# A graph-convolution kernel on one core: the first layer's product with its weights takes float16 halves instead of float32

## The reference, cut to what matters

```python
norm = rsqrt(deg_out[src] * deg_in[dst])
msg = (h[src] @ W1 + h[src] * h[dst] @ W2) * norm[:, None]
out = h @ W1 + segment_sum(msg, dst)
```

## Time and profile before

| | |
|---|---|
| median of 3 runs | 563.75 us (563.54 to 563.83) |
| the profiled execution's own time | 563.75 us |
| its span, first to last instruction | 559.7 us |
| busy: TensorE / VectorE / ScalarE | 493.3 / 423.7 / 247.3 us |
| first layer, first to last L667 | 245.2 to 401.7 us |
| second layer, first to last L673 | 405.5 to 555.6 us |

### The profile page before, as it was taken

One profiled execution on the slowest core, in us unless ns is written; L12 is line 12 of the kernel. 1 busy time (PEld: TensorE's weight loads), 2 busy tenths in 40 slices (PEclk: granted clock), 3 DMA queues, 4 the chain that ended last, 5 costly groups with the idle time before them and its releaser, 6 DMA issues.

```text
span 559.7 us, 19159 instructions
## 1 busy us (share of the span) xinstructions
PE 493.3 (88%) x7774; PEld 457.8 (82%) x7774; DVE 423.7 (76%) x1157; ACT 247.3 (44%) x661; POOL 192.4 (34%) x307
## 2 busy tenths in 40 slices
PE   0294688899797999599999999999999999999995
PEld 0073577687586877499999999999899999999995
DVE  4698469999888798777887787788766666767673
ACT  0285488899796888523223222322211111111111
POOL 3679698879999998400000000000000000000000
PEclk9998699999989799889999999999999999999999
DMA  2166110000000000000000000000000020002011
GB/s 69 52 102 113 53 30 19 7 19 3 19 3 20 2 21 2 1 2 3 3 2 2 4 2 2 2 4 2 3 1 2 4 40 2 3 2 39 3 26 18
DMA packets 19428, 9.87 MB, mean 18 GB/s; under 512 B 16081, under 2 KB 18657, under 8 KB 19342
## 3 DMA queue, kind: packets, MB, share of 16 engines
q1 hardware_dynamic: 18222, 5.93, 5.9%
q0 software_dynamic: 1120, 2.72, 1.9%
HBM read 5.19 MB, written 1.65 MB: 12 GB/s over the span
## 4 chain that ended last, share of the span: by engine, by line
PE 35%; DVE 22%; POOL 12%; issue 10%; ACT 6%; SPq 2%; DMA 1%; DVEq 0%; ACTq 0%; POOLq 0%
PE diff L789 25%; DVE mixed L583 8%; PE slab L737 5%; ACT h L870 2%; POOL hist L394 2%; DVE work L667 2%; PE diff L773 2%; SPq L344 2%; DVE work L645 2%; PE diff L720 2%; DVE work L651 2%; DVE work L654 2%; POOL h L454 2%; POOL words L397 2%; DVE los L547 2%
## 5 line engine op out<-in xcount | busy, mean ns | idle before, releaser
L547 DVE TENSOR_TENSOR los<-mixed,iota_bank 128x6144 bf16<-128x6144 bf16 x49 | 161.9, 3344 | 10.9 <-PE slab L737 10.9
L789 PE MATMUL diff<-los,mixed 128*128 128x129 f16 x2401 | 159.7, 222 | 6.3 <-DVE los L626 5.7
L789 PEld LDWEIGHTS diff<-los,mixed 128*128 128x128 fp8e4 x2401 | 153.4, 101 | 8.3 <-issue 5.8
L789 PE MATMUL diff<-late,mixed 128*128 128x128 f16 x2401 | 150.7, 219 | 1.1 <-DVE late L670 1.1
L789 PEld LDWEIGHTS diff<-late,mixed 128*128 128x128 fp8e4 x2401 | 145.6, 98 | 2.0 <-DVE late L670 0.7
L737 PEld LDWEIGHTS slab<-hots,los 128*128 128x128 bf16 x2352 | 123.8, 101 | 22.0 <-ACT saved L831 8.4
L737 PE MATMUL slab<-hots,los 128*128 128x98 fp8e5 x2352 | 130.6, 213 | 4.6 <-DVE los L547 4.4
L823 ACT ACTIVATE hots<-diff 128x784 f16<-128x784 f32 x147 | 118.0, 843 | 18.7 <-PE diff L720 18.6
L720 PE MATMUL diff<-select,mixed 80*128 80x392 f16 x294 | 70.7, 345 | 30.3 <-DMA mixed<-rows 18.0
L583 DVE TENSOR_SCALAR mixed<-words 128x400 int32<-128x400 int32 x294 | 90.4, 363 | 0.0
L397 POOL COPY words<-saved 128x392 uint16<-128x392 uint16 x98 | 84.6, 864 | 0.0
(11 more groups left out here) (126 smaller groups left out, 370.4 us busy)
## 6 DMA issues: line engine op xcount, KB each, us to landing
mixed<-rows SPq DMA_DIRECT2D x147, 12.0 KB, 1.8
x_sb<-in_x_dram SPq DMA_DIRECT2D x4, 384.0 KB
out_dram<-x_sb SPq DMA_DIRECT2D x8, 128.0 KB
los<-in_dst_dram SPq DMA_DIRECT2D x1, 750.0 KB
out_dram<-x_sb SPq DMA_DIRECT2D x4, 80.0 KB
out_dram<-x_sb SPq DMA_DIRECT2D x4, 48.0 KB
los<-samples,row_i POOLq DMA_INDIRECT x7, 2.7
wt<-in_L_gnn_W_dram SPq DMA_DIRECT2D x4, 16.0 KB, 2.1
```

The costliest lines, as they stand in the source:

```text
L547: nc.vector.tensor_tensor(out=los[:, b % LOS_RING].rearrange("e s (v t) -> e s v t", t=2), in0=key, in1=val, op=ALU.is_equal).then_inc(los ...
L789: ins = nc.tensor.matmul(acc[a][:, 0:width], tiles[:, a, q], parts[:, q, 0:width], start=(q == 0), stop=(q == BLOCKS - 1))
```

## The change

In the first layer the transposed row is kept as two float16 numbers per element, a high half and what rounding left. ScalarE writes the high half in place of the float32 copy, and VectorE, in a new step `low_turned`, subtracts it from the PSUM tile to make the low half. The weights are scaled by a power of two and split in the same way, once, at the end of `second_scale`. The product becomes four float16 matmuls in place of one float32 matmul. Since the weights now carry the scale, the one factor per block `rdi_sc1` becomes `rdi_rdo`, and a new factor `rdi_h` takes the scale out again for the new `h`. The second layer keeps its float32 product.

```diff
+                v(nc.vector.tensor_scalar(w0_scaled[:], wt[:, 0], scale1[:, 0:1], None, ALU.mult))
+                v(nc.vector.tensor_copy(w0_parts[:, 0], w0_scaled[:]))
+                v(nc.vector.tensor_tensor(out=w0_parts[:, 1], in0=w0_scaled[:], in1=w0_parts[:, 0], op=ALU.subtract))
...
-            nc.vector.tensor_scalar(rdo_sc1[:], rdo[:], scale1[:, 0:1], None, ALU.mult)
...
                     v(nc.vector.reciprocal(rdi[:, b:b + 1], root[:, b:b + 1]))
-                    v(nc.vector.tensor_tensor(out=rdi_sc1[:, b:b + 1], in0=rdi[:, b:b + 1], in1=rdo_sc1[:, b:b + 1],
+                    nc.vector.tensor_scalar(rdi_h[:, b:b + 1], rdi[:, b:b + 1], unscale1[:, 0:1], UNIT, ALU.mult,
+                                            ALU.mult).then_inc(h_scale, 1)
+                    v(nc.vector.tensor_tensor(out=rdi_rdo[:, b:b + 1], in0=rdi[:, b:b + 1], in1=rdo[:, b:b + 1],
                                               op=ALU.mult))
+            def low_turned(n):
+                a = n % 2
+                dve.wait_ge(t_hi_saved, n + 1)
+                nc.vector.tensor_tensor(out=halves_t[a][:, 1], in0=t_ps[a][:, 0:128], in1=halves_t[a][:, 0],
+                                        op=ALU.subtract).then_inc(t_lo_saved, 1)
...
             for n in range(POSITIONS + 1):
+                if 0 < n <= BLOCKS:
+                    low_turned(n - 1)
                 if n > 0:
                     finish(n - 1)
...
             def weigh(n):
                 a = n % 2
-                pe.wait_ge(t_saved, n + 1)
+                if n < BLOCKS:
+                    pe.wait_ge(t_lo_saved, n + 1)
+                else:
+                    pe.wait_ge(t_saved, n + 1 - BLOCKS)
...
-                nc.tensor.matmul(turn_z[a][:, 0:D], pair_t[a], wt[:, n // BLOCKS], start=True,
-                                 stop=True).then_inc(z_ready, 1)
+                if n < BLOCKS:
+                    for half in range(2):
+                        for part in range(2):
+                            ins = nc.tensor.matmul(turn_z[a][:, 0:D], halves_t[a][:, half], w0_parts[:, part],
+                                                   start=(half + part == 0), stop=(half + part == 2))
+                    ins.then_inc(z_ready, 1)
+                else:
+                    nc.tensor.matmul(turn_z[a][:, 0:D], pair_t[a], wt[:, 1], start=True, stop=True).then_inc(z_ready, 1)
...
-                nc.scalar.activation(pair_t[n % 2], t_ps[n % 2][:, 0:128], ACT.Copy).then_inc(t_saved, 1)
+                if n < BLOCKS:
+                    nc.scalar.activation(halves_t[n % 2][:, 0], t_ps[n % 2][:, 0:128], ACT.Copy).then_inc(t_hi_saved, 1)
+                else:
+                    nc.scalar.activation(pair_t[n % 2], t_ps[n % 2][:, 0:128], ACT.Copy).then_inc(t_saved, 1)
...
+                        act.wait_ge(h_scale, n)
                         nc.scalar.activation(h[:, n - 1], turn_z[(n - 1) % 2][:, 0:D], ACT.Relu,
-                                             scale=rdi[:, n - 1:n]).then_inc(z_used, 1)
+                                             scale=rdi_h[:, n - 1:n]).then_inc(z_used, 1)
```

More of the change, by code:

```diff
@@ L164, in fast_path @@
     unscale1 = sb("unscale1", [128, 1], FP32)
+    w0_parts = sb("w0_parts", [128, 2, D], FP16)
+    w0_scaled = sb("w0_scaled", [128, D], FP32)
     rdo = sb("rdo", [128, BLOCKS], FP32)
     rdo_sc0 = sb("rdo_sc0", [128, BLOCKS], FP32)
-    rdo_sc1 = sb("rdo_sc1", [128, BLOCKS], FP32)
     deg_in = sb("deg_in", [128, BLOCKS], FP32)
@@ L171, in fast_path @@
     rdi = sb("rdi", [128, BLOCKS], FP32)
-    rdi_sc1 = sb("rdi_sc1", [128, BLOCKS], FP32)
+    rdi_rdo = sb("rdi_rdo", [128, BLOCKS], FP32)
+    rdi_h = sb("rdi_h", [128, BLOCKS], FP32)
     totals = sb("totals", [128, 2], FP32)
@@ L208, in fast_path @@
     pair = [work_f[:, (6 + 2 * i) * D:(8 + 2 * i) * D].rearrange("p (k f) -> p k f", k=2) for i in range(2)]
+    halves_t = [work[:, (10 + 2 * i) * D:(12 + 2 * i) * D].bitcast(FP16).rearrange("p (k f) -> p k f", k=2) for i in range(2)]
     pair_t = [work_f[:, (10 + 2 * i) * D:(12 + 2 * i) * D] for i in range(2)]
@@ L277, in fast_path @@
     t_ready = sem("t_ready")
+    t_hi_saved = sem("t_hi_saved")
     t_saved = sem("t_saved")
+    t_lo_saved = sem("t_lo_saved")
+    h_scale = sem("h_scale")
     z_ready = sem("z_ready")
@@ L666, in finish @@
                         dve.wait_ge(hi1_ready, n - 1)
-                    nc.vector.tensor_scalar(g1[a], turn_z[a][:, 0:D], rdi_sc1[:, b:b + 1], 0.0,
+                    nc.vector.tensor_scalar(g1[a], turn_z[a][:, 0:D], rdi_rdo[:, b:b + 1], 0.0,
                                             ALU.mult, ALU.max).then_inc(g1_ready, 1)
@@ L759, in turn_pair @@
                 if n >= 2:
-                    pe.wait_ge(t_saved, n - 1)
+                    pe.wait_ge(t_hi_saved, min(n - 1, BLOCKS))
+                    pe.wait_ge(t_lo_saved, min(n - 1, BLOCKS))
+                if n - 2 >= BLOCKS:
+                    pe.wait_ge(t_saved, n - 1 - BLOCKS)
                 nc.tensor.transpose(t_ps[a][:, 0:128], pair[a].rearrange("p k f -> p (k f)"),
```

## The result

The changed kernel takes 597.23 us (596.12 to 597.37) beside 563.79 us of the kernel before: a ratio of 1.0585, with a 95% interval of 1.0565 to 1.0604. It is slower by 33.4 us. The forecast was 606.5, with a range from 598.5 to 614: the direction and the mechanism are as forecast, the size is not.

The account below looks back on a forecast made before the run. Two equally long loops, TensorE's and VectorE with ScalarE's, were taken to bound the 3.24 us round; it grows to 4.14, 47 times 0.90 plus the first and last rounds, 42.8 on 563.75: 606.5 us, range 598.5 to 614.

Parts of the forecast that it names:

- TensorE's round trip: First-layer product between `low_turned` and the next L667: restart 0.14 us after VectorE, four matmuls 47 ns apart, 0.21 to the end.
- the time outside the span: Profiled execution's time beyond its traced span, 563.75 against 559.7 us before; the forecast added 42.8 to the 563.75.
- What bounds the kernel: First-layer round of 3.24 us: TensorE's loop and the loop through VectorE and ScalarE equally long within about 0.05 us.
- The place of the step: `low_turned` stands behind `unpack` and ahead of `finish` on VectorE, so `unpack` and the product's round trip run one after the other.
- The restart: TensorE's first product matmul after waiting for VectorE's `low_turned`: 0.14 us after that instruction's end, other end 0.05.
- The rule on loads: Weight loads take columns over 1.2 GHz: four loads 107 ns apart, round 4.32, total 615 us; the sum kept 47 ns.
- The ends of the range: Rounds of 3.97 to 4.30 us, 47 times 0.73 to 1.06 more plus 0.45 for first and last rounds: 598.5 to 614.
- What is hidden: ScalarE's float16 copy (0.8 us of cover), the eight tiles behind the product, the transpose and the 0.03 cheaper product cost nothing.
- The weights' preparation: Three chained VectorE instructions behind block 8, 0.85 us in all, taken up by a 4.47 us wait for GpSimd.
- All covered: Rival, chance 0.05: VectorE reaches `low_turned` early enough, TensorE stays the limit and gains 0.03 us 49 times: 562.2 us.
- half covered: Rival, chance 0.05: the product's round trip overlaps other VectorE work, only new instructions count, 0.4 us a round: 583 us.
- The clock: Rival, chance 0.04: TensorE's short waits in each round lower its granted clock, its own round becomes 5.5 us: 672 us.

Follow-up runs that it names:

- the order that beats both kernels: Changed kernel's arithmetic reordered on VectorE in the first layer, unpack spread over its waits, one factor without its chained wait: 559.09 us, 0.9916 of the kernel before.
- The wait added alone: Kernel before, with the first layer's float32 product also waiting until VectorE has unpacked the tile two positions ahead; no instruction added: 591.79 us, ratio 1.0498.
- the swapped waits: Changed kernel with TensorE's two waits ahead of the product in the other order, `z_used` first, the low half second: 600.84 us.

## Why the prediction was right and wrong

The place of the cost was right. Two terms of the sum were too large, TensorE's round trip and the time outside the span, and the result lies below the range because of both: either one alone would have left it inside.

*What bounds the kernel* held: the two loops were equally long, and what went into VectorE's went into the round. In that order VectorE's lower busy share was no room; the order that beats both kernels made some of it usable. The wait added alone and the low half made twice show it.

*The place of the step* held. `low_turned` starts 3.32 after the last L683; the forecast had 3.33. Its duration, 0.28, was forecast as 0.29, and the factor's step, 302.39 to 302.52, as 0.12.

*TensorE's round trip* is the first step that failed. From the start of `low_turned` to the next L683 the forecast had 0.81 and the trace has 0.67, which is 0.14 to 0.15 in each of 47 rounds, some 7 us. Three terms of the sum share it. The restart was 0.14, from the earlier trace rows, and is 0.06. Behind that row stands a wait in a record of its own, at 398.70, as the swapped waits have it; the forecast's other end, 0.05, was nearly right. The three steps between the matmuls were 0.14, at 47 ns from the earlier trace rows, and are 0.10: that row has 98 columns, these matmuls 64, and the step goes with the columns. I had read it as the step of a 16-bit load of weights and set no bound below. The last matmul's own time was 0.21 and is 0.19.

*The rule on loads* would have put the matmuls 107 ns apart, an estimate after the Trainium skill, "TensorE: Matmul & The Clock Gate", section "LDWEIGHTS (loading the stationary operand)". They are some 30 ns apart here, so the trace disagrees with that spacing. It does not disagree much with the time of one load: each of these loads of 128 columns shows 95 to 99 ns (view of L800), but the next one starts while it still runs.

*The time outside the span* is the second step that failed. The forecast took it over from the kernel before as if it were a constant, 4.05; it is 1.7 here. The round of 3.99 lies just inside the forecast's 3.97 to 4.30, and with 4.05 outside the median would have been about 599.5, inside the range. With the forecast's round of 4.14 and 1.7 outside it would have been about 604, inside as well. The hundred memsets show that added instructions on VectorE move this time by as much without the float16 product; no row of the kernel before shows it.

*The ends of the range* do not follow from the bounds given. Added up, these are 0.06, 0.06 and 0.09 less and 0.07, 0.08 and 0.04 more, a round of 3.93 to 4.33 in place of 3.97 to 4.30. With 3.93 the range would have begun at 596.6 and held the result.

*What is hidden* held for ScalarE's copy (0.28, ended 0.84 before it was used), the transpose, the eight tiles and the cheaper product. The weights' preparation took 1.4 us in place of 0.85 and lay in the wait as said, but for the 1.1 us that stay open. At the end of the layer the last step took 0.14 more, where 0.3 was forecast. The first L683 comes 0.7 earlier than in the profile of before, and the first matmul of the products as well, so that is the start of the run and not this part.

*The rivals.* All covered and half covered fall: neither holds in the order of the changed kernel. Half covered is what the low half made earlier shows, 573.78 us. The clock stayed at 1.00 with a wait of 0.7 in every round, so the rule on frequent short waits, from the same page of the Trainium skill, section "A second HAM failure mode: psum-queue depth-cycling", does not come true here.

## What to carry to other kernels

Before work is added between two steps of one engine, write out the round from a fixed instruction to its next occurrence and see which loops close in it: an engine that is idle for a fifth of the time can still be the limit, and the place of an instruction in its program can cost more than the instruction (0.48 of 0.75 us here). If an operand has to pass through a third engine, put that step where the engine next comes free after its input is there, with other work left behind it to cover the way back; the same arithmetic then went from 597.23 to 559.09 us. And take a price from a row with the same shape and the same kind of wait, or keep the other end in the range.

## What the runs showed of the hardware

- The time outside the span went with the number of one engine's instructions, and not in one direction: 3.8 to 4.9 us with 1157 or 1160 instructions of VectorE, 1.6 to 2.1 with 1208 or 1257, 4.0 to 4.6 with 1306. A difference of 0.4% between two versions of this kernel can be this alone.
- Of two waits ahead of the product's first matmul, the one written second became an instruction of its own in these programs: when that was the one that came last, the restart took 0.15 us, otherwise 0.06.
- Four matmuls with full loads of 128 16-bit columns of weights went some 30 ns apart with 64 moving columns, and some 60 with 128, while each load shows 95 to 99 ns.
- A 128x64 float32 multiplication by a column took VectorE 0.89 us in the first stage, where one of the same shape out of PSUM takes 0.28 (L667). In each of the ten runs that have it, it ends 0.05 to 0.06 us after a copy of GpSimd's that runs beside it, whether it started with the copy or in the middle of it, so it lasts between 0.52 and 0.91. It looks held until GpSimd's copy is over; no run takes the copy away. The changed kernel first, then the run with the low half not awaited:

```profile
67.23 0.86 POOL L403 COPY words<-saved 128x392 uint16<-128x392 uint16 x1
67.25 0.89 DVE L578 TENSOR_SCALAR w_scaled<-wt,scale 128x64 f32<-128x64 f32 x1
...
68.06 0.84 POOL L403 COPY words<-saved 128x392 uint16<-128x392 uint16 x1
...
68.44 0.52 DVE L578 TENSOR_SCALAR w_scaled<-wt,scale 128x64 f32<-128x64 f32 x1
```
